# Decoder layer on one core: the self-attention queries are stacked with two batches side by side and 1088 bytes for each head

## The reference

```python
q, k, v = proj(Wq, bq), proj(Wk, bk), proj(Wv, bv)      # (batch, head, token, 8)
rk2, rv2 = rel_k[idx], rel_v[idx]                        # idx = clip(key - query, -20, 20) + 20
attn1 = einsum('bhqd,bhkd->bhqk', q, k)
attn2 = einsum('bhqd,qkd->bhqk', q, rk2)                 # the term called "bias" below
attn  = softmax((attn1 + attn2) / sqrt(8))
w = einsum('bhqk,bhkd->bhqd', attn, v) + einsum('bhqk,qkd->bhqd', attn, rv2)
x = layernorm(x + w @ Wo.T + bo)
# then the same with cross-attention (q from x, k and v from ctx, causal), then 8 experts, top 2, and a shared one
```

## Time and profile before

| What | Value |
|---|---|
| Median of 3 runs | 451.35 us |
| The profiled execution: its time / its span | 451.89 / 450.1 us |
| PE busy | 378.3 us, 84% |
| DVE busy | 303.4 us, 67% |
| ACT busy | 228.3 us, 51% |
| POOL busy | 80.0 us, 18% |
| Mean granted TensorE clock | 0.942 of full |
| PE's share of the chain that ended last | 54% (DVE 17%, DMA 10%) |

### The profile page before, as it was taken

How to read it: one execution, slowest core, us unless ns; L and a number is a source line. 1 busy time by engine, 2 the same in 40 slices (tenths; PEclk the granted TensorE clock), 3 DMA queues, 4 the chain that set the end, 5 groups by cost and what they waited for, 6 DMA issues and landing times.

```text
span 450.1 us, 11284 instructions
## 1 busy us (share of the span) xinstructions
PE 378.3 (84%) x4714; PEld 285.1 (63%) x4729; DVE 303.4 (67%) x630; ACT 228.3 (51%) x329; POOL 80.0 (18%) x92
## 2 busy tenths in 40 slices
PE   2556366974789999999999999999998989899992
PEld 1345234763566797767687976776685757566672
DVE  4246984469987679998775889998549476056324
ACT  2343046560069875326877853469944315844330
POOL 8910000020044012011131120003311202411001
PEclk9987559996989999999999999999999999999997
DMA  3261028724101360400112703010200310000100
GB/s 93 73 183 39 4 51 248 202 71 128 28 4 41 108 178 1 128 4 4 39 39 82 214 4 106 4 37 4 75 3 2 100 31 6 1 1 0 25 1 23
DMA packets 29420, 26.87 MB, mean 60 GB/s; under 512 B 12673, under 2 KB 27962, under 8 KB 28602
## 3 DMA queue, kind: packets, MB, share of 16 engines
q1 hardware_dynamic: 26042, 25.86, 20.7%
q10 hardware_dynamic: 3136, 0.27, 0.5%
q0 software_dynamic: 192, 0.03, 0.0%
HBM read 18.38 MB, written 7.35 MB: 57 GB/s over the span
## 4 chain that ended last, share of the span: by engine, by line
PE 54%; DVE 17%; DMA 10%; issue 6%; ACT 5%; SPq 5%; POOL 1%; POOLq 0%; DVEq 0%; ACTq 0%
PE ps_f L725 9%; PE ps_s L547 9%; PE ps_f L714 8%; PE ps_f L573 6%; PE ps_f L581 4%; DMA parts_by_head<-part 3%; PE ps_f L677 3%; PE ps_f L520 3%; DMA QS<-parts_by_head 3%; DVE ST L943 3%; PE ps_s L540 3%; DVE MX L946 3%; PE ps_s L556 2%; PE ps_f L526 2%; PE ps_s L636 2%
## 5 line engine op out<-in xcount | busy, mean ns | idle before, releaser
L547 PE MATMUL ps_s<-QS,KS 125*128 125x128 bf16 (+1 forms) x768 | 79.5, 249 | 11.9 <-DVE ST L943 6.6
L547 PEld LDWEIGHTS ps_s<-QS,KS 125*128 125x128 bf16 (+1 forms) x768 | 65.1, 106 | 34.6 <-DVE ST L943 9.0
L846 ACT ACTIVATE HT<-ps_f,hb 128x512 f32<-128x512 f32 x72 | 48.3, 688 | 74.0 <-PE ps_f L714 44.3
L725 PEld LDWEIGHTS ps_f<-w,HT 128*128 128x128 f32 x576 | 68.8, 192 | 8.1 <-issue 6.0
L725 PE MATMUL ps_f<-w,HT 128*128 128x128 f32 x576 | 72.1, 276 | 0.1
L714 PE MATMUL ps_f<-x2T,w 128*128 128x512 f32 x144 | 70.8, 602 | 1.4 <-DVE acc L1056 1.0
L488 POOL TENSOR_SCALAR_AFFINE_SELECT PC<-PC 128x1024 f32<-128x1024 f32 x32 | 34.8, 1094 | 142.2 <-ACT PC L810 142.2
L1060 DVE SCALAR_TENSOR_TENSOR acc<-ps_f,gw,acc 128x128 f32<-128x128 f32 x128 | 35.7, 341 | 21.8 <-PE ps_f L725 21.5
L810 ACT ACTIVATE PC<-ps_s 128x1024 f32<-128x1024 f32 x32 | 32.2, 1024 | 33.4 <-PE ps_s L547 30.1
L803 ACT ACTIVATE ST<-ST 128x1024 f32<-128x1024 f32 x32 | 33.9, 1061 | 28.0 <-DVE ST L974 27.6
L943 DVE TENSOR_TENSOR ST<-ps_s,ST 128x1024 f32<-128x1024 f32 x32 | 38.6, 1207 | 11.0 <-PE ps_s L547 10.9
(11 more groups left out here) (118 smaller groups left out, 525.2 us busy)
## 6 DMA issues: line engine op xcount, KB each, us to landing
parts_by_head<-part SPq DMA_DIRECT2D x16, 384.0 KB, 2.6
QS<-parts_by_head SPq DMA_DIRECT2D x24, 256.0 KB, 3.8
KS<-parts_by_head SPq DMA_DIRECT2D x24, 256.0 KB, 4.3
xin<-in_x SPq DMA_DIRECT2D x16, 64.0 KB, 2.7
cin<-in_ctx SPq DMA_DIRECT2D x4, 256.0 KB, 5.0
w<-in_L_ffn_rw SPq DMA_DIRECT2D x1, 1024.0 KB
out_x<-acc SPq DMA_DIRECT2D x16, 64.0 KB, 1.8
QS<-MP SPq DMA_DIRECT2D x32, 8.0 KB, 2.1
```

Source lines behind the costliest of these rows:

```text
L547: last = nc.tensor.matmul(ps[:, o:o + S], KS[a][0:kd, c:c + S], queries(a, kd, h, j), start=not masked and j == 0, stop=j == NB - 1, skip_ ...
L725: last = nc.tensor.matmul(ps[:, b * E:(b + 1) * E], HT[n % 2][:, f, b * S:(b + 1) * S], w2[:, e, f, :], start=f == 0, stop=f == NF - 1 and ...
L846: nc.scalar.activation(HT[n % 2][:, f, :], ps[:, :], ACT.Gelu, bias=hb[:, e, f:f + 1]).then_inc(ht_ready, 1)
```

## The change

In QS[0] a head gets 1088 bytes (Q_STEP = 544 bf16, of which 512 are used). Within a head there are first the tokens of batches 0 and 1, the two side by side, then those of batches 2 and 3: column = 544 h + 256 (b // 2) + 2 q + b % 2. What follows from it:

- p1 reads every second bf16 (4 bytes apart) where it read every fourth.
- bias reads runs of 2 bf16 where it read runs of 4. Its order is: for the first pair of batches all 16 heads, 1088 bytes apart, then the second pair. It writes to the same PSUM columns as before, now in steps: two columns, then two left out, and the others in the second round.
- ACT's high part and DVE's rest follow the new order of columns. DVE's instruction is split in two of 256 columns, for step q alone.
- st_q writes its rows head by head (16 x 16 x 512), because of the gaps. QS[1] and KS are as before.
- POOL's zeroing of QS[0] covers 8704 bf16 a row, not 8192.

```diff
+Q_HEAD = NB * S
+Q_STEP = Q_HEAD + 32
...
-        QS = [sb(f"QS{i}", [KD2, HB * S], BF16) for i in range(2)]
+        QS = [sb("QS0", [KD2, H * Q_STEP], BF16), sb("QS1", [KD2, HB * S], BF16)]
...
-                rows = spread[4 * ch + SLOT[what]].rearrange("e (d h) t -> (e d) (h t)", h=H)
+                rows = spread[4 * ch + SLOT[what]].rearrange("e (d h) t -> (e d) h t", h=H)
+                by_head = dst.rearrange("k (h t) -> k h t", h=H)[:, :, 0:Q_HEAD]
                 for c in range(0, NC, 2):
                     p = parts[c]
-                    sp.dma_start(dst[stack_rows(c, 2), :],
-                                 rows[p * HD:(p + 2) * HD, :]).then_inc(stacked[what], 16)
+                    sp.dma_start(by_head[stack_rows(c, 2), :, :],
+                                 rows[p * HD:(p + 2) * HD, :, :]).then_inc(stacked[what], 16)
...
-                return QS[0][0:kd, h * NB * S:(h + 1) * NB * S].rearrange("k (q b) -> k q b", b=NB)[:, :, b]
+                pair = h * Q_STEP + b // 2 * ST_PAIR
+                return QS[0][0:kd, pair:pair + ST_PAIR].rearrange("k (q b) -> k q b", b=2)[:, :, b % 2]
...
-            qs_q = QS[0][0:KZ, :].rearrange("k (h q b) -> k h q b", h=H, q=S)
+            qs_q = QS[0][0:KZ, :].rearrange("k (h t) -> k h t", h=H)[:, :, 0:Q_HEAD].rearrange(
+                "k h (c q b) -> k c h q b", c=2, b=2)
...
-                        last = nc.tensor.matmul(ps[:, j * HB:(j + 1) * HB], RK[0:KZ, S - 1 - q:2 * S - 1 - q],
-                                                qs_q[:, :, q, :], start=True, stop=True)
+                        last = nc.tensor.matmul(ps[:, j * HB:(j + 1) * HB].rearrange("p (h c b) -> p c h b", c=2, b=2),
+                                                RK[0:KZ, S - 1 - q:2 * S - 1 - q], qs_q[:, :, :, q, :],
+                                                start=True, stop=True)
...
-                        hi, src = hi.rearrange("p (q b) -> p q b", b=NB), src.rearrange("p (b q) -> p q b", b=NB)
+                        hi = hi.rearrange("p (c q b) -> p c q b", c=2, b=2)
+                        src = src.rearrange("p (c b q) -> p c q b", c=2, b=2)
...
-                        left, hi = (m.rearrange("p (q b) -> p q b", b=NB) for m in (left, hi))
-                        src = src.rearrange("p (b q) -> p q b", b=NB)
-                    nc.vector.scalar_tensor_tensor(left, src, bcol[:, b:b + 1], hi,
-                                                   ALU.add, ALU.subtract).then_inc(rest_ready[what], 1)
+                        left, hi = (m.rearrange("p (c q b) -> p c q b", c=2, b=2) for m in (left, hi))
+                        src = src.rearrange("p (c b q) -> p c q b", c=2, b=2)
+                        for c in range(2):
+                            last = nc.vector.scalar_tensor_tensor(left[:, c], src[:, c], bcol[:, b:b + 1], hi[:, c],
+                                                                  ALU.add, ALU.subtract)
+                        last.then_inc(rest_ready[what], 1)
+                    else:
+                        nc.vector.scalar_tensor_tensor(left, src, bcol[:, b:b + 1], hi,
+                                                       ALU.add, ALU.subtract).then_inc(rest_ready[what], 1)
```

## The result

| Kernel | median (lowest to highest) | ratio to before, 95% interval |
|---|---|---|
| before | 451.22 us (450.95 to 451.75, 4 runs) | |
| changed | 455.39 us (454.28 to 457.94, 4 runs) | 1.0109 (1.0071 to 1.0147) |
| changed, second comparison | 454.22 us (452.32 to 456.28, 7 runs) | 1.0086 (1.0056 to 1.0117), before there 450.48 |

The change makes the kernel slower, by 4.9 us in the first comparison and 3.9 in the second (1.0086 of 450.48). The forecast was 450.3 us and faster. The profiled execution was the slowest of the four: 457.94 us, span 456.2, mean clock 0.929 where before had 0.942. Between these single executions of nearly equal clock the change costs 451.9 - 450.1 = 1.8 us of span; how much of the rest is the clock stays open (last part of the explanation).

A forecast was written before the change was run, and what follows sets the result against it. Bounds: DVE in chunk 0's p1, ACT in chunk 1's bias, PE from chunk 2's bias on. Chunks 0 to 3 summed -0.26 - 1.32 - 0.12 + 0.6 = -1.1 us, from 451.35 to 450.3; own range 449.2 to 451.8, whole 442.5 to 457.

The forecast's parts named there:

- Reading (a): PE's strided reads are fetched in pieces of some bytes at one rate; p1 falls from 115 to 57.5 ns each.
- +128 x 27.8 = +3.56: Chunk 2's bias: all 128 matmuls are on the chain and lose 27.8 ns each, +3.56 us.
- +2.9: Chunk 3's bias loss in us, taken between 2.22 and 3.56 when pricing the slower rival.
- chunk 3's two counts: Chunk 3's net: +1.30 us by matmuls on the chain, -0.12 by PE's work; the middle, +0.6, was taken.
- -64 x 57.5 = -3.68: Chunk 2's p1: all 64 matmuls are on the chain and save 57.5 ns each, -3.68 us.
- 2 x 0.46 = -0.92: Chunk 1's p1: two of the tiles on the chain save 0.46 us each, within that chunk's -1.32 us.
- nothing, while ACT covers it: Bias in chunk 0: at most 0.92 us more a tile, hidden under ACT's 1.02 us copy; chunk 1's bias likewise.
- +0.20 us: DVE's split into two instructions of 256 columns, on the chain in chunk 0 ahead of the stack's DMAs: +0.20 us.
- rivals 2 and 4: Slower cases: p1 unchanged with bias slower, 458 us, chance 0.12; bias paying for gapped PSUM writes, 460 us, chance 0.08.
- Rival 2: In chunks 2 and 3, p1 stays at 115 ns while bias goes to 57.5: 458 us, chance 0.12.
- reading (b): PE's strided reads: an element without a neighbour costs double, whatever the step, so p1 stays at 115 ns.
- rival 3: Neither p1 (115 ns) nor bias (29.7 ns) moves, only DVE's 0.2 us is added: 451.6 us, chance 0.07.

The follow-up runs named there:

- bias2_23: Kernel before, with bias alone reading runs of 2 in chunks 2 and 3 only (wrong columns): 456.98 us, ratio 1.0142.
- the repeat: A profiled execution of the unaltered changed kernel from the second comparison: 453.62 us, span 451.9, mean clock 0.943.
- p1_all: Kernel before, with p1 alone reading every second element in all four chunks (wrong columns): 449.65 us, ratio 0.9967.
- p1_01: Kernel before, with p1 reading every second element in chunks 0 and 1 only (wrong columns): 451.44 us, ratio 0.9992.
- dve_p1: p1_all with DVE's p1 and p2 score additions handling half the columns: 439.49 us, against 443.52 for the kernel before with the same halving.
- bias2_all: Kernel before, with bias alone reading runs of 2 in all four chunks (wrong columns): 458.86 us, ratio 1.0178.
- after_1024: Changed kernel with 1024 bytes for each head instead of 1088, so no padding: 454.32 us, ratio 1.0077.
- pad_only: Kernel before with 1088 bytes for each head and st_q written head by head, reads otherwise as before: 450.86 us, ratio 0.9994.

## Why the prediction was wrong

- **Prices.** Right: p1 58.8 ns and bias 56.9 (57.5 forecast), DVE's halves 480 ns (478), gapped pairs in PSUM free, no effect seen of DMA pieces of 1 KB or of the padding. Reading (a) was the right one.
- **Chunks 2 and 3, bias.** Right: "+128 x 27.8 = +3.56" and +2.9 gave 6.5; bias2_23 measured 6.4. Of chunk 3's two counts PE's work was the better one: from its first bias to its first p1 matmul chunk 3 took 13.68 us before and 17.06 in the repeat, +3.4 of the 3.56 for all 128 matmuls, where the chain's 80 would give 2.2.
- **Failed step 1: p1's saving, "-64 x 57.5 = -3.68", "2 x 0.46 = -0.92" and their like, -7.8 in all, taken at full value.** Alone it is worth 1.5 us (p1_all), and in chunks 0 and 1 nothing (p1_01). That p1's matmuls stand on the chain of waits, and that PE had no gap, says that a longer p1 would cost in full; it doesn't say that a shorter one saves. The earlier trace rows held the limit: beside PE's 7.80 of 7.80 us in chunk 2's p1 stood DVE's 6.89, so of 7.80 us only 0.91 were free before DVE became the bound, and p1's matmuls in that stretch (16, and the first of the next 16) were to fall by more than 16 x 57.5 ns = 0.92 us. "What is late next: DVE under p1" was written down, but no price was put to it. dve_p1 shows the cause: with DVE relieved the same edit brings 4.0. It is the larger part and not the whole: what is left up to 7.8 is partly a wait for a DMA (0.71 us in chunk 2) and otherwise not placed.
- **The two halves are not independent.** With bias slow, p1's shorter step is worth about 8.0 - 3.9 = 4.1 us (bias2_all against the changed kernel, 1.0178 and 1.0086, intervals apart), against 1.5 alone. On bias2_all's own chip the same difference, to after_1024 (1.0077), is 4.5. In chunk 2 the traces show it as 1.9 against 0.8 us (the table of distances). A reason that fits: slow bias delays PE against DVE, which then enters the p1 stage with less work waiting. In the changed kernel's trace PE runs without a gap from 180 to 195 us and waits for acc later (0.28 and 0.81 us); in p1_all it waits from 181 us on. The size is measured, the reason is argued: no run isolates it.
- **Failed step 2: bias in chunks 0 and 1, "nothing, while ACT covers it".** Measured +2.4 (1.1 to 3.7). 0.92 us under a 1.02 us copy held between tiles that follow each other, but not for the last tile, nor in chunk 1, where PE has other work between the tiles: its stage took 8.0 to 8.5 us with fast bias (pad_only, before) and 9.5 to 10.4 with slow (the repeat, the first profile). Of that 0 to 2.5 us reached p1, by when bias started. The rest of the 2.4 goes with a lower clock, and which of the two brings about the other isn't shown.
- **DVE's split, "+0.20 us", counted in full.** The duration of one half is right, but on the chain the two take 0.89 us together where the whole instruction took 0.76: +0.13. No run isolates its effect on the time, and it is under what can be told.
- **Sum.** -7.8 for p1 became -4.1, and 6.5 for bias became 8.0: 8.0 - 4.1 = 3.9 us, which is what the second comparison measured (the 4.1 is itself from that difference, so this is an account and no check; a check of the 8.0 is 2.4 + 6.4 = 8.8).
- **The range.** The forecast's own, 449.2 to 451.8, doesn't follow from its two sources: 450.3 with 0.7 and 0.5 us each way is 449.1 to 451.5. The whole range, up to 457, holds the measured 454.2 and 455.4, but by luck: it reached so far for rivals 2 and 4, and both fell. Rival 2 was also wrongly priced: in bias's runs of 2 every element has a neighbour, so reading (b) leaves bias at 29.7 ns and gives rival 3's time, not 458.
- **Open.** The first comparison's median is 1 us above the second's, with intervals that overlap. The four runs there go with their granted clock (0.943, 0.940, 0.938 and 0.929 with 454.28, 455.65, 455.13 and 457.94 us), but the clock's lower stretches differ between executions of every kernel here, before too. Whether the changed kernel draws more of them isn't settled; in the second comparison its seven runs have a mean clock of 0.940 and the 18 of before 0.938.

No version here with all of DVE's work beats before by more than p1_all's 1.5 us, and p1_all multiplies other pairs than the reference. The reason is one of bytes: p1 wants one batch's neighbouring tokens in a 16-byte piece, bias one token's batches; of the piece's 8 elements with two batches side by side p1 uses 4 and bias 2, with four it is 2 and 4. The product is 8 either way. A second copy of the stack, one for each reader, wasn't tried.

## What to carry to other kernels

Count the 16-byte pieces that each reader of a shared layout touches, and make the reader whose engine has no cover the cheap one: here p1 has DVE at its heels, and bias in chunks 2 and 3 hasn't. Before a saving is counted, put beside it the slack of the next engine in that stretch (its length minus that engine's busy time): a loss on a full engine costs its whole size, a gain at most that slack. It is a bound and no forecast: from 172.26 to 193.75 us before's DVE was busy 19.75 of 21.49 us, 1.74 free, and p1_all took 21.42 us for the same work. And a step that is hidden under a copy of about the same length isn't hidden in its last tile, nor where its engine has other work between the tiles.

## What the runs showed of the hardware

- Moving bf16 columns at full clock cost 1.7 to 1.8 ns for each 16-byte piece touched, at least 29 ns for 64 columns: 29.7, 58.4 and 115 ns for 4, 2 and 1 elements in a piece. The Trainium skill's "SBUF — State Buffer", section "Door 1: The DMA port swizzle", gives full bandwidth from two hits in 16 bytes on; here it took four, and the measurement decides. Successive runs that share a piece paid for it once (33 ns against 57).
- PSUM written in pairs with gaps cost nothing (28.8 ns), one column in four 54.4. By the Trainium skill's "Advanced Engine Details and Errata", section "Memory Cachelines", every two consecutive elements should be together: the trace agrees. That section also has the harder sentence of "PSUM — Partial Sum Buffer", section "Specifications (TRN2)", that any access that is not contiguous slows matmuls significantly: it does not hold here for pairs.
